# Last layer of a decoder: expert outputs scattered to their token's row, read back by plain reads, and the last unit finished tile by tile

## Chip, core and metric

One core of a Trainium2 chip runs the whole program. The metric is the device time of one execution in microseconds (us).

## The reference

A decoder of four layers, each of self-attention, cross-attention and an expert feed-forward, with a residual sum and a layer norm after each. There are 8 batches of 256 tokens, 2048 tokens of 256 float32 values. The change touches only the last part, the feed-forward of layer 3:

```python
x_flat = x.reshape(T, D)                                   # 2048 x 256
shared = jnp.einsum('th,hd->td', silu(x_flat @ shared_w1.T), shared_w2.T)   # hidden size 1024
gate_logits = x_flat @ gate_w.T                            # 8 experts
top_k_gates, top_k_idx = jax.lax.top_k(gate_logits, 2)
top_k_gates = jax.nn.softmax(top_k_gates, axis=1)
...
selected = jnp.einsum('ted,te->td', expert_out, gates)     # two chosen experts per token
x = _layernorm(x + shared + selected)
```

## The kernel before

`experts_sparse` computes the shared expert for all tokens and each of the 8 experts only for the tokens that chose it. The work is a list of 31 units q. A unit multiplies 256 rows with the up weights (four PSUM banks, 48 matmuls on line 3308, each float32 product made of three products of a high and a low part), applies silu (ScalarE), splits the result into high and low parts hH and hL (VectorE; in the last units ScalarE makes hH), and multiplies with the down weights (48 matmuls, line 3334) into a bank named y.

- Units 0 to 3 are the shared expert on batches 0 to 3. While they run, VectorE works out the routing: `choose`, `place`, `mark_tiles`, `mark_slots`, `find_tokens`. Each of a token's two choices gets a slot in one of 23 blocks of 256 slots; 32 small products on TensorE (`sources`, line 3269) turn that around into a list of the token of each slot.
- Units 4 to 26 are the 23 blocks, each with the weights of one expert. POOL gathers the rows of a block with two indirect DMAs (`fetch`, line 3453). VectorE copies the finished y to SBUF (`take_y`, line 3629) and SP stores it as a whole in DRAM in the order of the slots (`store_block`, line 3216).
- Units 27 to 30 are the shared expert on batches 4 to 7 ("late" units).

The weights of a unit (two loads of 1 MB by SP, up and down) are also split: ScalarE writes the high parts upH and downH (lines 3352, 3358), POOL the low parts upL and downL (`low`, lines 3441, 3444). SP starts the load of the weights after next when the low part has been made.

At the end each token needs its two block rows back. POOL waits until all blocks are stored, then issues 32 indirect gathers by slot (line 3483), one per tile of 128 tokens and choice, four to a batch. On VectorE `complete(b)` waits for a batch's four gathers, adds the rows with their gate weights (lines 3606, 3607) and makes the layer norm's statistics; POOL makes the power for the deviation (`power`, line 3473), ScalarE applies both in `finish(b)` (lines 3374, 3379), and SP stores the batch (line 3230). The batches are completed in pairs after the splits of units 28, 29 and 30 (`completed`), and batches 6 and 7 after unit 30's y has been taken:

```python
take_y(NQ - 1)
freed(dve, ("y", NQ - 1))
for b in range(2 * (B - FRONT - 1), B):
    complete(b)
```

All engines run their own program in order; the order is written out by hand, with semaphores between the engines. A wait holds all that stands behind it on that engine.

Of the kernel before, what the change touches and what calls it, by code (L numbers as in the profile page):

```python
# [3085 lines left out]
class Sparse:  # L3086


    def __init__(self, nc, g, scope, other, raw):
# [12 lines left out]
        self.yg = [raw[i // 16][:, D * (i % 16):D * (i % 16 + 1)] for i in range(2 * NT)]  # L3102
# [22 lines left out]
        self.source = sb("slot_tokens", TILES, U32)  # L3125
        self.chosen = sb("chosen", 136, BF16)
# [5 lines left out]
def experts_sparse(nc, g, name, n, scope):  # L3132
# [10 lines left out]
    rows_x, slots_y = g.dram["rows_x"], g.dram["slots_y"]  # L3143
# [15 lines left out]
    def completed(l):  # L3159

        return range(2 * (l - 1), 2 * l) if 1 <= l < B - FRONT else range(0)
# [11 lines left out]
    for q in range(NQ):  # L3173
        for f in range(4):
            u.add(("u", q, f), f)
        if q == 0:
            u.add("tokens", 6), u.add("rank", 7), u.add("count", 6)
        if q == FRONT - 1:
            u.add("source", 7)
        if q + 1 < NQ and block_of(q + 1) is not None:  # L3180
            u.add(("xT", q + 1), 6 + q % 2)
        u.add(("y", q), 4 + q % 2)

# [12 lines left out]
    with nc.Block() as block:  # L3196
        @block.sync
        def _(sp):
# [15 lines left out]
            def store_block(j):  # L3214
                freed(sp, ("y", FRONT + j))
                sp.dma_start(slots_y[j * S:(j + 1) * S, :].rearrange("(t p) d -> p t d", p=P), m_.yb[j % 2].rearrange("p (t d) -> p t d", d=D))\
                    .then_inc(g.block_stored[j % 2].sem, 16)
# [10 lines left out]
            for b in range(B):  # L3228
# [3 lines left out]
            sp.wait_ge(g.out_stored.sem, 16 * B)  # L3232

        @block.tensor
        def _(pe):
# [56 lines left out]
            for q in range(NQ):  # L3292
# [32 lines left out]
                split(pe, g.down_low, w)  # L3325
                to = claim(("y", q))
# [12 lines left out]
        def _(act):  # L3339
# [56 lines left out]
            for q in range(NQ):  # L3396

                after = weights_of(q) + 1 if last_unit(weights_of(q)) == q and weights_of(q) + 1 < SETS else None
                hidden(q, 0)
                hidden(q, 1)  # L3400
                if q == 2:
                    act.wait_ge(g.places_ready.sem, g.places_ready.base + 1)
                    nc.scalar.activation(m_.tile_row.rearrange("p (i c) -> p i c", c=2 * TILES)[:, :, 0:TILES],
                                         m_.at_tile.rearrange("p (i c) -> p i c", c=TILES), ACT.Copy, scale=m_.row).then_inc(g.places_ready.sem, 1)
# [19 lines left out]
            for b in range(2 * (B - FRONT - 2), B):  # L3424
                finish(b)

        @block.gpsimd
        def _(pool):
# [42 lines left out]
            def power(b):  # L3471
                pool.wait_ge(g.var_ready.sem, g.var_ready.base + b + 1)
                nc.gpsimd.tensor_tensor(g.rstd[:, 2 * b:2 * b + 2], g.vare[:, 2 * b:2 * b + 2], g.mhalf[:, 0:2], ALU.pow).then_inc(g.rstd_ready.sem, 1)


            split(pool, g.up_low, SETS - 1)
            split(pool, g.down_low, SETS - 1)
            for parity in range(2):
                sig = g.block_stored[parity]
                pool.wait_ge(sig.sem, sig.base + 16 * ((SLOTS + 1 - parity) // 2))  # L3480
# [7 lines left out]
            for b in range(2, B):  # L3488
                power(b)

        @block.vector
        def _(dve):
# [65 lines left out]
            def mark_tiles():  # L3558
# [18 lines left out]
            def find_tokens():  # L3577
# [4 lines left out]
                                                    in1=m_.found[:, 0:TILES], op1=ALU.add))  # L3582
                nc.vector.tensor_copy(m_.source[:, :], m_.token).then_inc(g.slots_ready.sem, 1)
# [19 lines left out]
            def add_choices(t):  # L3603

                r = rows(t)
                step(nc.vector.scalar_tensor_tensor(out=r, in0=m_.yg[2 * t], scalar=w1[:, t:t + 1], op0=ALU.mult, in1=r, op1=ALU.add))  # L3606
                nc.vector.scalar_tensor_tensor(out=r, in0=m_.yg[2 * t + 1], scalar=w2[:, t:t + 1], op0=ALU.mult, in1=r, op1=ALU.add)\  # L3607
                    .then_inc(g.added.sem, 1)

            def complete(b):  # L3610
                dve.wait_ge(g.gathered[b].sem, g.gathered[b].base + 64)
                add_choices(2 * b)
                add_choices(2 * b + 1)
                dve.wait_ge(g.added.sem, g.added.base + 2 * b + 2)
                normalize_part1(nc, g, dve, lambda t: rows(2 * b + t), 2, 2 * b, step, None)
                nc.vector.tensor_scalar(g.negmax[:, 2 * b:2 * b + 2], g.meanvar[:, 4 * b:4 * b + 4].rearrange("p (t two) -> p t two", two=2)[:, :, 0],
                                        -1.0, None, ALU.mult).then_inc(g.centered.sem, 1)

            def take_y(q):
# [5 lines left out]
                else:  # L3625
                    if j >= 2:
                        sig = g.block_stored[j % 2]
                        dve.wait_ge(sig.sem, sig.base + 16 * (j // 2))
# [3 lines left out]
            for q in range(NQ):  # L3632
# [19 lines left out]
                if q + 1 < NQ and block_of(q + 1) is not None:  # L3652
# [3 lines left out]
                        .then_inc(g.freed[u.bank(key)].sem, 1)  # L3656
                for b in completed(late(q)):
# [323 lines left out]
def decoder(nc, dram, out, order):  # L3981
# [3 lines left out]
    dram["slots_y"] = nc.dram_tensor("slots_y", (SLOTS * S, D), F32, kind="Internal").ap()  # L3985
# [213 lines left out]
```

## Time and profile before

| | us |
|---|---|
| median of three runs | 3414.25 |
| lowest, highest | 3413.76, 3416.06 |
| profiled execution, first to last instruction (span) | 3419.0 |
| TensorE busy in the span | 3115.7 (91%) |
| VectorE, ScalarE, POOL busy | 1875.7, 1705.1, 1520.5 |

Of the profiled execution only the span is known; it is 4.75 us longer than the median of the runs without a profile. Times in the rows count from the span's start. The feed-forward of the last layer takes from about 2980 to the end. PE is TensorE, PEld its weight loads, DVE VectorE, ACT ScalarE, POOL GpSimd, SPq the queue of SyncE.

### The profile page before, as it was taken

How to read it: one execution, taken by the hardware profiler on the slowest of the kernel's cores; microseconds unless marked ns; L12 is line 12 of the kernel's file. 1: busy time of each engine (PE TensorE's matmuls, PEld its weight loads, DVE VectorE, ACT ScalarE, POOL GpSimd, SP SyncE). 2: the span in 40 equal slices, each digit the busy share in tenths (PEclk: the TensorE clock that was granted, in tenths of full speed). 3: DMA queues.
4: the chain of work that ended last, by engine and by line, in shares of the span. 5: the costliest groups of instructions: out<-in, count | busy, mean ns of one | idle time of the engine just before them, and what ended most of it. 6: DMA issues, size and time to landing. Idle time of an engine off the chain costs nothing. (4 is left out here: it accounts for less than half of the span.)

```text
span 3419.0 us, 59989 instructions
## 1 busy us (share of the span) xinstructions
PE 3115.7 (91%) x23982; PEld 2628.8 (77%) x23993; DVE 1875.7 (55%) x3913; ACT 1705.1 (50%) x3695; POOL 1520.5 (44%) x1146
## 2 busy tenths in 40 slices
PE   6997999999698898998997989799997999889995
PEld 5776888888575565897665868678886888789995
DVE  4764222223566465776554754467775666565554
ACT  4763332332276554554654653356665666535553
POOL 0222344434212675674234651233334454539984
PEclk9998999999799999999998999899999999999998
DMA  1002000100000010442001010110001000036652
GB/s 65 3 11 79 19 19 19 38 1 1 23 3 23 1 50 1 149 168 75 3 3 43 8 50 1 39 50 1 1 1 38 6 6 1 26 115 217 223 181 74
DMA packets 49794, 156.96 MB, mean 46 GB/s; under 512 B 9322, under 2 KB 29438, under 8 KB 37104
## 3 DMA queue, kind: packets, MB, share of 16 engines
q1 hardware_dynamic: 45776, 142.90, 12.2%
q0 software_dynamic: 3744, 10.23, 1.0%
q8 instruction: 194, 3.18, 0.4%
q14 instruction: 80, 0.66, 0.1%
HBM read 142.06 MB, written 10.26 MB: 45 GB/s over the span
## 5 line engine op out<-in xcount | busy, mean ns | idle before, releaser
L1303 POOL TENSOR_TENSOR prob<-prob,inv 128x512 f32<-128x512 f32 x320 | 331.6, 1042 | 401.3 <-DVE inv L1355 391.8
L1193 ACT ACTIVATE prob<-banks,nmax 128x256 f32<-128x256 f32 x640 | 297.3, 474 | 155.1 <-DVE nmax L1349 155.0
L2682 POOL TENSOR_TENSOR hL<-product,hH 128x512 fp32r<-128x512 f32 x128 | 165.9, 1296 | 321.5 <-ACT hH L2629 321.5
L2288 DVE TENSOR_REDUCE nmax<-banks 128x4 f32<-128x1024 f32 (+1 forms) x192 | 217.5, 1133 | 153.7 <-PE banks L1870 85.9
L2727 DVE TENSOR_TENSOR product<-banks,silu 128x512 f32<-128x512 f32 x128 | 88.6, 692 | 388.6 <-PE banks L2553 333.4
L2621 ACT ACTIVATE silu<-banks 128x512 f32<-128x512 f32 x128 | 76.5, 598 | 367.6 <-PE banks L2553 367.6
L1349 DVE TENSOR_REDUCE nmax<-banks 128x2 f32<-128x512 f32 x320 | 215.4, 685 | 20.6 <-PE banks L1172 16.2
L2553 PE MATMUL banks<-xH,upH 128*128 128x512 f32 x512 | 202.1, 395 | 5.8 <-POOL upL L2669 5.8
L2553 PE MATMUL banks<-xL,upH 128*128 128x512 f32 x512 | 201.5, 394 | 0.0
L2553 PE MATMUL banks<-xH,upL 128*128 128x512 f32 x512 | 199.9, 390 | 0.0
L3364 ACT ACTIVATE banks<-banks 128x512 f32<-128x512 f32 x124 | 71.9, 584 | 213.9 <-PE banks L3308 186.8
L1093 PE MATMUL bank<-ident,prob 128*128 128x128 f32 x1280 | 167.8, 274 | 6.6 <-POOL prob L1303 6.6
L1093 PEld LDWEIGHTS bank<-ident,prob 128*128 128x128 f32 x1280 | 148.9, 141 | 21.8 <-issue 4.9
L2158 POOL TENSOR_TENSOR res<-res,bcast 128x512 f32<-128x512 f32 x16 | 21.4, 1337 | 313.7 <-DVE res L2356 313.7
L2105 ACT ACTIVATE probT<-banks 128x1024 f32<-128x1024 f32 (+1 forms) x129 | 123.2, 955 | 71.0 <-PE banks L1988 39.8
L3308 PE MATMUL banks<-xH,upH 128*128 128x256 f32 x496 | 142.7, 288 | 7.7 <-issue 7.7
L3308 PE MATMUL banks<-xH,upL 128*128 128x256 f32 x496 | 142.4, 287 | 6.7 <-issue 6.5
L3334 PE MATMUL bank<-downH,hH 128*128 128x256 f32 x496 | 143.7, 290 | 4.4 <-DVE hL L3648 4.3
L3308 PE MATMUL banks<-xL,upH 128*128 128x256 f32 x496 | 142.8, 288 | 3.2 <-issue 3.2
L2571 PE MATMUL bank<-downH,hL 128*128 128x256 f32 x512 | 144.9, 283 | 0.0
L2571 PE MATMUL bank<-downL,hH 128*128 128x256 f32 x512 | 144.8, 283 | 0.0
L2571 PE MATMUL bank<-downH,hH 128*128 128x256 f32 x512 | 144.4, 282 | 0.0
(617 smaller groups left out, 11026.6 us busy)
## 6 DMA issues: line engine op xcount, KB each, us to landing
W<-in_L_ffn_experts SPq DMA_DIRECT2D x80, 1024.0 KB, 5.4
W<-in_L_ffn_experts SPq DMA_DIRECT2D x8, 1536.0 KB, 7.9
slots_y<-W SPq DMA_DIRECT2D x23, 256.0 KB, 6.1
W<-strips SPq DMA_DIRECT2D x4, 768.0 KB, 7.5
W<-in_L_ffn_experts SPq DMA_DIRECT2D x9, 256.0 KB, 4.9
X<-in_x SPq DMA_DIRECT2D x1, 2048.0 KB, 8.3
cs<-in_ctxT SPq DMA_DIRECT2D x16, 128.0 KB, 2.3
W<-in_L_ffn_experts SPq DMA_DIRECT2D x1, 2048.0 KB, 7.6
```

Source lines behind the costliest of these rows:

```text
L1093: mm = nc.tensor.transpose(to[:, kt * S + qt * P:kt * S + (qt + 1) * P], m_.prob[p % 2][:, c0:c0 + P], ident[:, :])
L1193: ins = nc.scalar.activation(m_.prob[p % 2][:, e * 512 + j * S:e * 512 + (j + 1) * S], bank(key)[:, j * S:(j + 1) * S], ACT.Exp, bias=m_.n ...
L1303: nc.gpsimd.tensor_tensor(pr, pr, m_.inv[:, slot(p, e):slot(p, e) + 2].unsqueeze(2).to_broadcast([P, 2, S]), ALU.mult)\
L1349: nc.vector.tensor_reduce(m_.nmax[:, slot(p, e):slot(p, e) + 2], sc, AX.X, ALU.max, negate=True).then_inc(g.max_ready.sem, 1)
L2105: nc.scalar.activation(heads(m_.probT[(8 * b + i) % 3]), heads(g.pairs[1]), ACT.Exp)\
L2288: nc.vector.tensor_reduce(m_.nmax[b % 2][:, 2 * parts * i_:2 * parts * (i_ + 1)].rearrange("p (e q) -> p e q", e=2), scores.rearrange("p e ...
L2553: mm = nc.tensor.matmul(to[:, :], w_[e % 2][:, c0:c0 + P], x_[:, x0:x0 + 512], start=(at == 0), stop=(at == 5))
L2571: mm = nc.tensor.matmul(to, h_[:, c0:c0 + P], w_[e % 2][:, f * D:(f + 1) * D], start=(f == 0 and t % 2 == 0 and at == 0), stop=(f == 3 and ...
L2682: nc.gpsimd.tensor_tensor(m_.hL[:, at], m_.product[s % 2][:, :], m_.hH[:, at].bitcast(F32), ALU.subtract).then_inc(g.h_low.sem, 1)
L2727: nc.vector.tensor_tensor(m_.product[s % 2][:, :], bank(("u", s))[:, :], m_.silu[s % 2][:, :], ALU.mult)\
L3308: mm = nc.tensor.matmul(to[:, (f % 2) * S:(f % 2 + 1) * S], w_[w % 2][:, kk * 1024 + f * P:kk * 1024 + (f + 1) * P], x_[:, x0:x0 + S], sta ...
L3334: mm = nc.tensor.matmul(to[:, t * D:(t + 1) * D], h_[:, c0:c0 + P], w_[w % 2][:, f * D:(f + 1) * D], start=(f == 0 and t == 0 and at == 0) ...
```

## The change

1. **Scatter instead of store.** The list of slots gives for each slot its place as well, token + 2048 x choice (empty slots go to 128 spare rows). `mark_tiles` and `find_tokens` work this out. SP's store of a block and POOL's 32 gathers go. For each block POOL issues two indirect scatters, `scatter(j, 0)` and `scatter(j, 1)`, from SBUF to `rows_y` in DRAM. Each waits until the one before has landed.
2. **Plain reads.** When the last scatter has landed, SP issues sixteen reads of 256 KB, two for a batch, into the space of the weights.
3. **downL to VectorE.** The low part of the down weights is made by VectorE after its splits of a unit, no longer by POOL.
4. **Order of the end.** Batch 0 is completed in unit 27, 1 and 2 in unit 28, 3 and 4 in 29, 5 and 6 in 30. In unit 30 TensorE makes the down products one tile of 128 tokens after the other, in two banks. VectorE has the choices of the last two tiles added beforehand and finishes each tile with `end_tile`; SP stores the two tiles apart.
5. **ScalarE** no longer makes a factor of the routing product in unit 2; VectorE makes it.

The diff, cut to its core:

```diff
-        return range(2 * (l - 1), 2 * l) if 1 <= l < B - FRONT else range(0)
+        return range(max(2 * l - 1, 0), 2 * l + 1) if 0 <= l < B - FRONT else range(0)
...
+            def load_choices(b):
+                for k in range(2):
+                    sp.dma_start(m_.yg[b][:, 2 * k * D:2 * (k + 1) * D].rearrange("p (t d) -> p t d", d=D),
+                                 rows_y[k * T + b * S:k * T + (b + 1) * S, :].rearrange("(t p) d -> p t d", p=P)).then_inc(g.gathered[b].sem, 16)
             for w in range(1, SETS):
                 load_weights(w)
-                if w >= 4:
-                    store_block(w - 4)
-            for j in range(SETS - 4, SLOTS):
-                store_block(j)
+            split(sp, g.up_low, SETS - 1)
+            split(sp, g.down_low, SETS - 1)
+            for parity in range(2):
+                sig = g.block_stored[parity]
+                sp.wait_ge(sig.sem, sig.base + 32 * ((SLOTS + 1 - parity) // 2))
+            for b in range(B):
+                load_choices(b)
...
+                if q == NQ - 1:
+                    for t, key in enumerate((("y", q), "last")):
+                        to = claim(key)
+                        for f in range(8):
...
+                        done(key, mm)
+                    continue
...
-                split(pool, g.down_high, w)
-                nc.gpsimd.tensor_tensor(m_.downL[w % 2][:, :], raw[w % 2][:, 2048:4096], m_.downH[w % 2][:, :].bitcast(F32), ALU.subtract)\
-                    .then_inc(g.down_low.sem, 1)
+            def scatter(j, t):
+                if t == 0:
+                    freed(pool, ("y", FRONT + j))
+                    if j:
+                        sig = g.block_stored[(j - 1) % 2]
+                        pool.wait_ge(sig.sem, sig.base + 32 * ((j + 1) // 2))
+                else:
+                    sig = g.block_stored[j % 2]
+                    pool.wait_ge(sig.sem, sig.base + 32 * (j // 2) + 16)
+                i = 2 * j + t
+                nc.gpsimd.indirect_dma_start(rows_y, bass.IndirectOffsetOnAxis(ap=m_.place[:, i:i + 1], axis=0),
+                                             m_.yb[j % 2][:, t * D:(t + 1) * D], None).then_inc(g.block_stored[j % 2].sem, 16)
...
             for w in range(1, SETS):
                 low(w)
+                if w >= 3:
+                    scatter(w - 3, 1)
                 if w + 1 < SLOTS:
                     fetch(w + 1)
+                if w >= 2:
+                    scatter(w - 2, 0)
+            scatter(SLOTS - 1, 1)
...
-            for t in range(NT):
-                for k in range(2):
-                    nc.gpsimd.indirect_dma_start(m_.yg[2 * t + k], None, slots_y,
-                                                 bass.IndirectOffsetOnAxis(ap=m_.slots[:, k * NT + t:k * NT + t + 1], axis=0))\
-                        .then_inc(g.gathered[t // 2].sem, 16)
-                if t in (9, 11):
-                    power(t // 2 - 4)
...
-                for k in range(2):
-                    half = slice(k * NT, (k + 1) * NT)
-                    nc.vector.tensor_tensor(each(m_.tile_row, 2 * TILES)[:, half, TILES:2 * TILES], each(m_.at_tile, TILES)[:, half, :],
-                                            m_.count[:, 0:NT].unsqueeze(2).to_broadcast([P, NT, TILES]), ALU.mult)
+                nc.vector.tensor_scalar(m_.offset[:, :], m_.low, m_.row, None, ALU.subtract)
+                step(nc.vector.tensor_scalar(m_.choice[:, :], m_.count[:, 0:2 * NT], float(2 * NT), None, ALU.subtract))
+                for part, factor in enumerate((m_.offset, m_.choice)):
+                    ins = nc.vector.tensor_tensor(each(m_.tile_row, 2 * TILES)[:, :, part * TILES:(part + 1) * TILES], each(m_.at_tile, TILES),
+                                                  factor[:, :].unsqueeze(2).to_broadcast([P, 2 * NT, TILES]), ALU.mult)
+                ins.then_inc(g.places_ready.sem, 1)
...
-                nc.vector.tensor_copy(m_.source[:, :], m_.token).then_inc(g.slots_ready.sem, 1)
+                step(nc.vector.tensor_scalar(m_.token, m_.token, m_.row, float(2 * T), ALU.add, ALU.add))
+                step(nc.vector.tensor_copy(m_.place[:, :], m_.token))
+                nc.vector.tensor_scalar(m_.source[:, :], m_.place[:, :], T - 1, None, ALU.bitwise_and).then_inc(g.slots_ready.sem, 1)
...
+            def end_tile(t, key, n_):
+                filled(dve, key)
+                step(nc.vector.tensor_tensor(rows(t), bank(key)[:, 0:D], rows(t), ALU.add))
+                normalize_part1(nc, g, dve, lambda _: rows(t), 1, t, step, None)
+                dve.wait_ge(g.rstd_ready.sem, g.rstd_ready.base + n_ + 1)
+                normalize_part2(nc, g, lambda _: rows(t), 1, t, lambda _: g.X[:, t * D:(t + 1) * D]).then_inc(g.x_done.sem, 1)
...
+                after = next_weights(q)
+                if after is not None:
+                    split(dve, g.down_high, after)
+                    nc.vector.tensor_tensor(m_.downL[after % 2][:, :], raw[after % 2][:, 2048:4096], m_.downH[after % 2][:, :].bitcast(F32), ALU.subtract)\
+                        .then_inc(g.down_low.sem, 1)
                 for b in completed(late(q)):
                     complete(b)
-            take_y(NQ - 1)
-            freed(dve, ("y", NQ - 1))
-            for b in range(2 * (B - FRONT - 1), B):
-                complete(b)
+            dve.wait_ge(g.gathered[B - 1].sem, g.gathered[B - 1].base + 32)
+            for t in (NT - 2, NT - 1):
+                step(add_choices(t, g.X[:, t * D:(t + 1) * D]))
+            end_tile(NT - 2, ("y", NQ - 1), B - 1)
+            end_tile(NT - 1, "last", B)
```

## Rows read from the trace of the kernel before

**Rows 1.** The page's first line.

```profile
span 3419.0 us, 59989 instructions
```

**Rows 2.** Windows, units 27 to 30: busy us by engine, TensorE clock, DMA share, GB/s.

```profile
3329.86:3341.38 11.52, 11.52 (x99) 11.52 (x98) 3.37 (x5) 4.33 (x8) 8.95 (x8) 1.00 0.26 81
3341.38:3371.44 30.06, 16.50 (x99) 14.95 (x98) 6.49 (x17) 4.15 (x8) 13.21 (x15) 0.72 0.23 66
3371.44:3383.34 11.90, 11.78 (x98) 11.58 (x98) 8.74 (x22) 7.70 (x16) 9.67 (x10) 1.00 0.29 79
3383.34:3401.60 18.26, 13.85 (x96) 13.08 (x95) 10.55 (x34) 8.12 (x18) 5.81 (x8) 0.91 0.26 80
```

**Rows 3.** Chain that ended last, 3330 to the end: start us, us, what.

```profile
3335.62 5.76 PE bank L3334 x48
...
3356.23 2.43 issue
...
3390.00 5.58 PE banks L3308 x35
...
3413.12 0.40 ACTq L3196
```

**Rows 4.** POOL's timeline, first and last of the twenty and of the twelve gathers.

```profile
3333.75 0.96 POOL L3483 DMA_INDIRECT W<-slots_y,slots  x1 [0.74 <-POOL downL L3444]
...
3357.54 0.95 POOL L3483 DMA_INDIRECT W<-slots_y,slots  x1 [0.30 <-issue]
3371.38 0.97 POOL L3473 TENSOR_TENSOR rstd<-vare,mhalf 128x2 f32<-128x2 f32 x1 [12.89 <-DVE vare L307]
3372.53 1.03 POOL L3483 DMA_INDIRECT W<-slots_y,slots  x1 [0.19 <-issue]
...
3387.67 0.96 POOL L3483 DMA_INDIRECT W<-slots_y,slots  x1 [0.30 <-issue]
```

**Rows 5.** Timelines of VectorE and ScalarE: what ended their long waits.

```profile
3360.10 0.69 DVE L3624 TENSOR_TENSOR W<-bank,X 128x512 f32<-128x512 f32 x1 [22.03 <-remote]
...
3362.29 1.07 ACT L3364 ACTIVATE banks<-banks 128x512 f32<-128x512 f32 x2 [25.06 <-remote]
```

**Rows 6.** Windows: plain traffic at its thickest, and one block unit.

```profile
2183.00:2186.00 3.00, 3.00 (x19) 2.88 (x18) 0.69 (x1) 1.17 (x2) 0.14 (x1) 0.76 1.06 388
...
3246.40:3258.35 11.95, 11.95 (x103) 11.95 (x102) 6.72 (x10) 6.35 (x7) 11.15 (x5) 1.00 0.67 218
```

**Rows 7.** VectorE's timeline in mark_tiles.

```profile
3027.29 1.69 DVE L3565 TENSOR_TENSOR W<-W 128x1472 bf16<-128x1472 f32 x1
3029.01 1.76 DVE L3570 TENSOR_TENSOR W<-W 128x736 bf16<-128x736 bf16 x2
```

**Rows 8.** DMA issues, last number us to landing: whole program; 3330 to 3340.

```profile
slots_y<-W SPq DMA_DIRECT2D x23, 256.0 KB, 6.1
...
slots_y<-W SPq DMA_DIRECT2D x1, 256.0 KB, 2.1
```

**Rows 9.** Groups on POOL, 3060 to 3330.

```profile
L3441 POOL TENSOR_TENSOR upL<-W,upH 128x2048 fp32r<-128x2048 f32 x23 | 106.7, 4638 | 12.2 <-ACT upH L3352 12.1
```

**Rows 10.** Timelines: VectorE beside a POOL operation and without one; a later gather.

```profile
1834.61 2.76 DVE L1400 TENSOR_TENSOR woL<-W,woH 128x1024 fp32r<-128x1024 f32 x1 [4.47 <-ACT woH L1243]
...
1833.91 2.36 POOL L1280 TENSOR_TENSOR wvL<-W,wvH 128x1024 fp32r<-128x1024 f32 x1
...
2610.18 1.23 DVE L1400 TENSOR_TENSOR woL<-W,woH 128x1024 fp32r<-128x1024 f32 x1 [1.70 <-ACT woH L1243]
...
3382.26 1.13 POOL L3483 DMA_INDIRECT W<-slots_y,slots  x1 [0.30 <-issue]
```

**Rows 11.** VectorE's timeline: last splits of unit 27; complete(5), and what follows it.

```profile
3336.78 1.29 DVE L3648 TENSOR_TENSOR hL<-banks,hH 128x512 fp32r<-128x512 f32 x2 [0.75 <-ACT hH L3368]
...
3401.15 0.48 DVE L3606 SCALAR_TENSOR_TENSOR W<-W,small 128x256 f32<-128x256 f32 x1
...
3404.37 0.68 DVE L3624 TENSOR_TENSOR W<-bank,X 128x512 f32<-128x512 f32 x1
```

More of the change, by code:

```diff
@@ L3100, in __init__ @@
         self.yb = [other[:, 5120:5632], other[:, 5632:6144]]
-        self.yg = [raw[i // 16][:, D * (i % 16):D * (i % 16 + 1)] for i in range(2 * NT)]
+        self.yg = [raw[b // 4][:, 4 * D * (b % 4):4 * D * (b % 4 + 1)] for b in range(B)]
         self.xbH, self.xbL = ([a.rearrange("p (k t) -> p k t", k=2)[:, :, i * S:(i + 1) * S] for i in range(2)] for a in (g.xH, g.xL))
@@ L3125, in __init__ @@
         self.source = sb("slot_tokens", TILES, U32)
+        self.place = sb("slot_places", TILES, U32)
+        self.offset, self.choice = sb("row_offsets", 2 * NT, F32), sb("choice_tiles", 2 * NT, F32)
         self.chosen = sb("chosen", 136, BF16)
@@ L3182, in experts_sparse @@
         u.add(("y", q), 4 + q % 2)
+    u.add("last", 4 + NQ % 2)
     def bank(key):
@@ L3222, in _ @@
                 load_weights(w)
-                if w >= 4:
-                    store_block(w - 4)
-            for j in range(SETS - 4, SLOTS):
-                store_block(j)
+            split(sp, g.up_low, SETS - 1)
[5 more added lines that the diff above has]
+                load_choices(b)
             out = g.dram["out"]
-            for b in range(B):
+            for b in range(B - 1):
                 sp.wait_ge(g.finished.sem, g.finished.base + b + 1)
@@ L3325, in _ @@
                 split(pe, g.down_low, w)
+                if q == NQ - 1:
+                    for t, key in enumerate((("y", q), "last")):
+                        to = claim(key)
+                        for f in range(8):
+                            if t == 0 and f % 2 == 0:
+                                freed(pe, ("u", q, f // 2))
+                            c0 = f * S + t * P
+                            for at, (h_, w_) in enumerate(((m_.hH, m_.downH), (m_.hH, m_.downL), (m_.hL, m_.downH))):
+                                mm = nc.tensor.matmul(to[:, 0:D], h_[:, c0:c0 + P], w_[w % 2][:, f * D:(f + 1) * D],
+                                                      start=(f == 0 and at == 0), stop=(f == 7 and at == 2))
+                        done(key, mm)
+                    continue
                 to = claim(("y", q))
@@ L3423, in _ @@
                     down_high(after)
-            for b in range(2 * (B - FRONT - 2), B):
+            for b in completed(B - FRONT - 1):
                 finish(b)
@@ L3467, in _, with power @@
                 low(w)
+                if w >= 3:
+                    scatter(w - 3, 1)
                 if w + 1 < SLOTS:
                     fetch(w + 1)
[L3471 to L3480, printed above, removed]
-            for t in range(NT):
-                for k in range(2):
-                    nc.gpsimd.indirect_dma_start(m_.yg[2 * t + k], None, slots_y,
-                                                 bass.IndirectOffsetOnAxis(ap=m_.slots[:, k * NT + t:k * NT + t + 1], axis=0))\
-                        .then_inc(g.gathered[t // 2].sem, 16)
-                if t in (9, 11):
-                    power(t // 2 - 4)
-            for b in range(2, B):
-                power(b)
+                if w >= 2:
+                    scatter(w - 2, 0)
+            scatter(SLOTS - 1, 1)
+            def power(i, t0, tiles):
+                pool.wait_ge(g.var_ready.sem, g.var_ready.base + i + 1)
+                nc.gpsimd.tensor_tensor(g.rstd[:, t0:t0 + tiles], g.vare[:, t0:t0 + tiles], g.mhalf[:, 0:tiles], ALU.pow).then_inc(g.rstd_ready.sem, 1)
+            for b in range(B - 1):
+                power(b, 2 * b, 2)
+            power(B - 1, NT - 2, 1)
+            power(B, NT - 1, 1)
         @block.vector
@@ L3601, in rows, with add_choices @@
                 return m_.R[:, t * D:(t + 1) * D]
[L3603 to L3608, printed above, removed]
+            def add_choices(t, onto):
+                r, yg = rows(t), m_.yg[t // 2]
+                first, second = (yg[:, (2 * k + t % 2) * D:(2 * k + t % 2 + 1) * D] for k in range(2))
+                step(nc.vector.scalar_tensor_tensor(out=r, in0=first, scalar=w1[:, t:t + 1], op0=ALU.mult, in1=onto, op1=ALU.add))
+                return nc.vector.scalar_tensor_tensor(out=r, in0=second, scalar=w2[:, t:t + 1], op0=ALU.mult, in1=r, op1=ALU.add)
             def complete(b):
[L3611 to L3614, printed above, removed]
+                dve.wait_ge(g.gathered[b].sem, g.gathered[b].base + 32)
+                add_choices(2 * b, rows(2 * b))
+                step(add_choices(2 * b + 1, rows(2 * b + 1)))
                 normalize_part1(nc, g, dve, lambda t: rows(2 * b + t), 2, 2 * b, step, None)
```

26 lines of the change are left out of this document (12 added, 14 removed).

## Prediction

> **What bounds the kernel now.** I began with the page's span [rows 1] and cut the end of the last layer into its units with the windows view [rows 2]. In the twenty-three block units before it TensorE is busy all the time: 11.95 us of each 11.95 [rows 6]. The first of the four last units, 27, still takes 11.52 us. Then unit 28 takes 30.06, unit 29 11.90, and unit 30 with what follows it 18.26; busy time is only 16.50 of the 30.06, and the granted clock falls to 0.72. Against 11.52 for a unit, unit 28 loses 18.5 us.
>
> The chain of waits says how [rows 3]. TensorE leaves the down products of unit 27 on time, and then its matmuls come one by one with up to 2.43 us of "issue" between them: it waits for nothing that the profile shows. The timeline of POOL shows what runs beside it [rows 4]: twenty indirect gathers, one each 1.25 us from 3333.75 to 3358.5. TensorE flows again only when ScalarE wakes, at 3362.3 [rows 5]. A second run of twelve gathers, 3372.53 to 3388.6, has the same beside it: single matmuls until 3390.00, where the next full piece of the chain begins, which ends at 3395.6. VectorE and ScalarE are late by the same wait [rows 5]: they wait 22.03 and 25.06 us for signals of TensorE and wake at 3360.10 and 3362.29, though unit 27's products were over at 3341.4. So the stall is on TensorE's side, and it lasts as long as the gathers. TensorE loses time in two places: 18.5 us in unit 28, and 6.5 us in the up products of unit 30 (3383.34 to 3395.6, where 5.76 is usual); unit 29 loses 0.4. Together 25.4 us.
>
> **The change part by part.**
>
> *Gathers out, plain reads in.* The 32 gathers at the end (4.2 MB) go, and sixteen reads of 256 KB from SP take their place. What plain traffic does to TensorE is read where it is thickest while TensorE works: at 2183 to 2186 the DMA engines are full (share 1.06, 388 GB/s), and TensorE is busy 3.00 of 3.00 us while its clock is just rising (0.76 granted) [rows 6]. In a block unit 218 GB/s cost nothing. So I price the stall in the new kernel at 0; the other end is that the reads hold TensorE back while they run, 4.2 MB at 388 GB/s = 11 us. I take 0, since these rows are of the same queue and kind. That gives TensorE 25.4 us back; how much reaches the end is worked out below.
>
> *When the reads come.* Unit 26's products end at 3329.86 [rows 2] and are taken 0.7 us later, two scatters follow each other's landing (the store without other traffic lands in 2.1 us [rows 8]), so SP starts its reads near 3339, and the first batch's two land by 3341.9. VectorE is done with unit 27 at 3338.07 [rows 11] and waits in complete(0) some 4 us. Behind it stand take_y(27) and the splits of unit 28, which TensorE wants only from 3347; the delay is hidden, with nearly 1 us to spare. If the reads came 5 us later, TensorE would pay about 4.
>
> *Tiles of the routing.* mark_tiles has at_tile of 1472 elements at 1.69 us and two halves of 736 in 1.76 together, with the other factor done by ScalarE. Now VectorE makes two products of 1472: 3.4 us for 1.76, and two small steps of 0.17 [rows 7]. VectorE runs without a gap there up to the mark that the source products of TensorE wait for, so all of it is on the path: +2.0 us. Two more small steps in find_tokens, 0.4 us, delay the first fetches, which land before unit 3's up products end: 0 to 0.4.
>
> *downL to VectorE.* 23 subtractions leave POOL, each the size of the one that takes 4.64 us [rows 9]. On VectorE 1024 elements took 1.23 us with POOL idle [rows 10], so 2048 take 2.3. VectorE is busy 6.72 of 11.95 us in a block unit; 9.0 still fit, and the new work stands behind its splits and before take_y, whose bank is one of two. Nothing of it is on the path.
>
> *Scatters in a loop with POOL.* This is the term with two sides. Each unit POOL now has upL (4.64 us [rows 9]), scatter (j,1), two fetches, and scatter (j+1,0), which waits until scatter (j,1) has landed; the next upL stands behind it. The loop is landing + 0.96 of issue [rows 4] + 4.64 + 0.2 for two signals (an estimate) = landing + 5.8. It may take 11.95. A transfer queued beside a 1 MB weight load landed in 6.1 us (median of 23 stores), without one in 2.1 [rows 8]. SP issues the next weights right beside scatter (j,1), so 6.1 is the nearer row: the loop is 11.9, equal to the unit. I take 0 cost, and keep +0.5 us a unit above (a landing of 6.6; 22 units less the 1.9 us by which upL is early now, an estimate from the timeline of such a unit: it ends near 10.0 us of the unit, and the next up products start at 11.95: +9) and nothing below, as TensorE is full.
>
> The Trainium skill, page "DMA: Bandwidth & Descriptors", section "Anatomy of one DMA — SWDGE (gpsimd) path", fits a GpSimd DMA at about 2.0 us and bytes over 436 GB/s, 2.3 us for a scatter's 128 KB; by that the loop would be an estimated 8.1 us and this risk gone. The rows differ: 2.1 us holds only with no load in the queues.
>
> *The end.* With no stall TensorE ends up products of unit 30 at 3329.86 + 3 x 11.52 + 5.76 = 3370.2, plus 2.0 for the routing = 3372.2. VectorE's splits end 2.45 us after the up products (3338.07 against 3335.62 in unit 27 [rows 3, 11]): 3374.6. Then it does complete(5) and (6), 3.22 us each (3401.15 to 3404.37 [rows 11]): 3381.1; the choices of the last two tiles, four of 0.48 to 0.49: 3383.1. Unit 30's products by tile end near 3375.5 and 3378.4, so TensorE no longer sets the end: VectorE does. A last tile costs the addition 0.48, its share of the statistics 0.9 (3.22 less four additions leaves 1.27 for two tiles), POOL's power 0.97 [rows 4], the normalisation 0.48: 2.8, twice, in series: 3388.7. From the last X to the end of the span are 5.5 us (ScalarE's last signal at 3413.52 [rows 3], span 3419.0): 3394.2.
>
> The sum: 3419.0 to 3394.2, -24.8 us, of the profiled execution. It is nearly the stall: what the tiles gain behind TensorE's last product pays for the +2.0. The profiled execution's span is 4.75 us longer than the median of 3414.25. If nothing of the stall is the profiler's, the time is 3414.25 - 24.8 = 3389.5; if these 4.75 us lie in the stall, it is 3394.2. I take 3392.
>
> **The rivals.**
>
> *The stall belongs partly to the profiled execution.* For it: only TensorE is held, which fills more of the records than any other engine, and the span is above the median. Without the stall the old order ends so: VectorE has complete(4) and (5) from 3372.6, take_y, complete(6) and (7), until 3386.5, ScalarE 1.9, then 5.5: 3394, as the new one. So the change would be worth nothing: 3414. Against it: the median is only 4.75 us under the span. A half-real stall gives 3402.
>
> *The reads hold TensorE as the gathers did*, for their 11 us: 3403. Rows 6 speak against it.
>
> *POOL becomes the bound.* One mechanism, on the other side: scatter (j,1) lands later than 6.1 us, and every unit grows. Each microsecond costs 22. The gain of 22 is eaten when the unit grows by 1.1 us, from a landing near 7.2; at 8 us the loop is 13.8: 22 x 1.85 - 1.9 = +39, and with the gain of 22 the time is 3431. For it: the store's 6.1 is a median under one load. Against it: the scatter stands in a queue of its own, ahead of the fetches.
>
> *The lock between VectorE and POOL.* With two SBUF inputs, a VectorE subtraction that began 0.7 us into a POOL one took 2.76 us, ending 1.1 after it [rows 10]; a gather that began beside a VectorE addition took 1.13 us where 0.95 is usual [rows 10, 4]. So downL starts when upL ends, and scatter (j,1), due at that instant, may wait its 2.3 us. The weight load ahead of it hides this as far as I can see; if not, the loop is 14.2: 22 x 2.2 - 1.9 = +47, time 3439.
>
> The Trainium skill states such an exclusive lock in "SBUF — State Buffer", section "Who interferes with whom", for a VectorE instruction with two SBUF inputs against a GpSimd one that reads SBUF; by that rule the trace agrees for the subtraction.
>
> **How the numbers follow.** My forecast (gathers' stall gone, 3386 to 3398): 0.62. Stall partly or wholly the profiler's: 0.14, of which 0.10 without change. Reads hold TensorE: 0.06. POOL's loop costs under 15 us: 0.06, near the gain (no change) 0.03, more 0.05. The lock: 0.04. Faster by over 0.2% (6.8 us, about what a measurement of this kernel can tell): 0.62 + 0.04 + 0.06 + 0.05 = 0.77, lowered to 0.75 as these cases can add up; no change 0.14; slower 0.11. For 8 in 10 I leave out the slow loop and the lock above and little below: 3385 to 3414. The forecast's own range is 3386 to 3398.
>
> **What would show it.** Right: no "issue" waits of TensorE above 1 us after 3340; units 27 to 30 at 11.5 us each; sixteen reads from SP near 3341 that land by 3360; mark_tiles 2.0 us longer; VectorE as the last link, two single tiles in series at the end. POOL's upL begins as soon as upH is there (its wait names ScalarE): if its wait names a DMA, the loop has closed, and the block units show more than 11.95 us. VectorE's downL should last 2.3 to 3.2 us, the scatters 0.96 or, with the lock, up to 3.2. The prediction is wrong if plain reads stall TensorE, if the block units grow, or if the old stall was cheaper without the profiler.

## The result, and the profile after

| | before | after |
|---|---|---|
| median | 3415.15 (4 runs, 3413.76 to 3419.5) | 3450.5 (4 runs, 3443.09 to 3460.82) |
| profiled execution, span | 3419.0 | 3459.0 |
| last layer: SP's store of rows_x to the end of the span | 3419.0 - 2979.45 = 439.6 | 3459.0 - 2982.16 = 476.8 |

After over before is 1.0108, interval [1.0087, 1.0129]: the change made the kernel slower by 1.1%. In the profiled executions the last layer grew by 37.2 us. I forecast 24.8 less.

The first thing to see is where TensorE is busy. Windows of the kernel after: 240 us of block units, then most of the down products of unit 27 with the up products of unit 28, the next two such pairs, and the end (columns as in [rows 2]):

```profile
3060.00:3300.00 240.00, 212.76 (x1695) 210.18 (x1694) 201.99 (x188) 107.97 (x119) 168.52 (x81) 0.96 0.51 184
...
3401.18:3412.70 11.52, 10.20 (x87) 10.03 (x85) 5.62 (x16) 4.34 (x9) 1.04 (x2) 1.00 0.66 210
3412.70:3424.45 11.75, 11.75 (x98) 11.75 (x99) 9.33 (x28) 4.74 (x10) 1.63 (x2) 1.00 0.57 188
3424.45:3435.98 11.53, 11.53 (x98) 11.53 (x98) 9.39 (x28) 7.74 (x16) 1.62 (x2) 1.00 0.13 45
3435.98:3459.00 23.02, 6.02 (x48) 5.61 (x47) 12.86 (x41) 8.61 (x19) 2.95 (x4) 0.73 0.17 58
```

Behind the block units TensorE runs nearly as forecast. SP issues the sixteen reads from 3403.38 on, and beside them (210 and 188 GB/s in the window) TensorE is busy but for one wait of 1.3 us, which is for VectorE; before had 16.50 of 30.06 [rows 2]. But in the block units it is busy 212.76 of 240, where it was always busy [rows 6]. From one upL to the next, a **round** of POOL, are 14.82 us on average, not 11.95. Groups of the block units, 3060 to 3390, POOL and then VectorE (to be held against [rows 9]):

```profile
L3464 POOL TENSOR_TENSOR upL<-W,upH 128x2048 fp32r<-128x2048 f32 x23 | 109.8, 4772 | 8.0 <-ACT upH L3379 7.4
L3478 POOL DMA_INDIRECT rows_y<-W,slot_places x43 | 76.9, 1789 | 82.7 <-DMA rows_y<-W,slot_places 78.9 <-issue 3.8
```

```profile
L3699 DVE TENSOR_TENSOR downL<-W,downH 128x2048 fp32r<-128x2048 f32 x23 | 114.6, 4983 | 0.4 <-ACT downH L3385 0.4
```

POOL stands 78.9 us ahead of its scatters and the releaser is the landing of a scatter. Only 3 of the 23 upL still wait for upH (7.4 us together); in [rows 9] nearly all of POOL's wait ahead of them was for upH. A scatter takes 1.79 us on the mean, downL 4.98, where 0.96 and 2.3 were put in. The timelines show why. POOL:

```profile
3194.22 4.58 POOL L3464 TENSOR_TENSOR upL<-W,upH 128x2048 fp32r<-128x2048 f32 x1
3198.96 2.87 POOL L3478 DMA_INDIRECT rows_y<-W,slot_places  x1 [0.17 <-issue]
3202.14 0.98 POOL L3487 DMA_INDIRECT W<-rows_x,slot_tokens  x1 [0.30 <-issue]
3203.42 0.96 POOL L3487 DMA_INDIRECT W<-rows_x,slot_tokens  x1 [0.30 <-issue]
3207.96 1.01 POOL L3478 DMA_INDIRECT rows_y<-W,slot_places  x1 [3.58 <-DMA rows_y<-W,slot_places]
3209.00 5.87 POOL L3464 TENSOR_TENSOR upL<-W,upH 128x2048 fp32r<-128x2048 f32 x1
```

VectorE, and SP's weight loads, at the same time:

```profile
3193.70 7.25 DVE L3699 TENSOR_TENSOR downL<-W,downH 128x2048 fp32r<-128x2048 f32 x1
3208.22 2.28 DVE L3699 TENSOR_TENSOR downL<-W,downH 128x2048 fp32r<-128x2048 f32 x1
```

```profile
3198.96 0.33 SPq L3217 DMA_DIRECT2D W<-in_L_ffn_experts  x1
3201.12 0.33 SPq L3220 DMA_DIRECT2D W<-in_L_ffn_experts  x1
```

Read them side by side. downL starts while the scatter ahead of upL is still being issued, 0.5 us before upL, and ends only at 3200.95, 2.15 us after upL: nearly the whole of its 2.28 us was done when upL was over. So while upL ran, downL did not. Scatter (j,1), due at 3198.96, is in turn held until 3201.83. The end of downL also frees SP's down load, issued at 3201.12. So the scatter, whose issue is over at 3201.83, stands behind two loads of 1 MB; before, these were issued 4.6 us apart (SP at 3197.13 and 3201.74). The next scatter starts at 3207.96, 9.0 us after scatter (j,1) was due and 6.1 after its issue was over. Then 1.0 and upL, and the round has 14.8 us. In a few other rounds, as that of 3209, downL gets through first, upL takes 5.87, the scatter 1.0, and both loads are issued within 0.5 us; from this scatter to the next are 7.4 to 8.8 us. Over all rounds the median is 8.8. TensorE is late behind upL: the view of waits for 3060 to 3390 puts 42.4 us of "issue" ahead of its up products.

The end, VectorE's last tile and SP's last lines:

```profile
3449.19 0.42 DVE L3653 TENSOR_TENSOR W<-bank,W 128x256 f32<-128x256 f32 x1
...
3451.20 0.41 DVE L313 TENSOR_SCALAR X<-W,meanvar,rstd 128x256 f32<-128x256 f32 x1 [0.67 <-POOL rstd L3512]
```

```profile
3403.38 10.31 SPq L3225 DMA_DIRECT2D W<-rows_y  x16
3414.75 32.45 SPq L3242 DMA_DIRECT2D out<-X  x7
3449.31 2.69 SPq L3246 DMA_DIRECT2D out<-X  x2
```

From one last tile's X to the next are 2.33 us (3448.87 to 3451.20), where I put 2.8. But from the last X (3451.61) to the end are 7.4 us, not 5.5; the experiments show why.

### The profile page after: what moved, and what is told of

Same layout as the page of the kernel before. It is cut to its first block and busy times, and to the rows that moved or that the text cites. A ratio compares the mean times of both kernels' runs of the same rounds, so it can differ in the third digit from the quotient of the medians.

```text
span 3459.0 us, 60033 instructions
## 1 busy us (share of the span) xinstructions
PE 3127.8 (90%) x23993; PEld 2641.1 (76%) x23993; DVE 1995.3 (58%) x3945; ACT 1701.0 (49%) x3690; POOL 1467.1 (42%) x1137
## 5 line engine op out<-in xcount | busy, mean ns | idle before, releaser
L3323 PE MATMUL banks<-xH,upH 128*128 128x256 f32 x496 | 148.8, 300 | 42.4 <-issue 42.4
```

The lines of the kernel that those rows point to most:

```text
L3323: mm = nc.tensor.matmul(to[:, (f % 2) * S:(f % 2 + 1) * S], w_[w % 2][:, kk * 1024 + f * P:kk * 1024 + (f + 1) * P], x_[:, x0:x0 + S], sta ...
```

## The experiments

They ran in three groups on two chips. On these, 73 runs of before lie between 3378.5 and 3400.4, where the runs of the prediction and the result gave 3413.8 to 3419.5. Which chip those first runs used is not on record; below they are "the first chip", though it is not shown that the chip itself makes the difference. Ratios are each against before in the same group. The store of rows_x in the last layer comes at 2968.5 to 2982.2 us in the profiles, a spread of some 14 us that comes from the layers that are the same in all kernels. So beside the time stands the **stretch** of the profiled execution, from that store to the end of the span. Before has 414.2 and 414.2 on the two chips and the kernel after 476.8 and 473.7, so I take differences of 2 to 3 us between two stretches with care.

**e1_quarters: the lock split.** downL as four subtractions of 512 columns, so that POOL gets in between.

```diff
-                    nc.vector.tensor_tensor(m_.downL[after % 2][:, :], ...)
+                    for c in range(0, 2048, 512):
+                        ins = nc.vector.tensor_tensor(m_.downL[after % 2][:, c:c + 512], ...)
```

> Edit: VectorE makes downL in four pieces of 512 columns instead of one operation of 2048; all else as in the changed kernel. Lock theory (VectorE's downL keeps POOL's scatter (j,1) from starting, 2.87 us instead of 0.97 in most units, and this delay is what makes the loop longer than 11.95 us): a piece holds POOL back only about 0.6 us, the scatter takes at most 1.6 us, a block unit shrinks by 1.3 us or more, from 14.7 to 13.4 or less, and the time falls by 25 us or more, to 3425 or less. Queue theory (scatter (j,1) lands late because both weight loads of 1 MB, which SP now issues 2.2 us apart, are served before it): the scatter starts earlier but lands no earlier, units stay at 14.2 to 14.7, the time stays within 10 us of 3450.

Measured 3402.13 us, ratio 1.0043 [1.0026, 1.006]; stretch 423.8, round 12.39 us. Scatter (j,1) takes 1.3 us, and from its issue to the next scatter the median is 6.3 us, not 8.8. The lock theory had the direction, but this edit does not separate the two: the scatter's issue is now over before SP starts the down load (3166.79 against 3167.89 in one round), so one load less stands ahead of it as well.

**e2_down_late and e3_loads_late: the loads moved.** SP starts the down load (e2), or both (e3), only when scatter (j,1) has landed. downL is whole. The edit of e3; e2 has the same wait ahead of the down load instead:

```diff
+                if w >= 5:
+                    sp.wait_ge(g.block_stored[(w - 5) % 2].sem, g.block_stored[(w - 5) % 2].base + 32 * ((w - 5) // 2 + 1))
                 sp.dma_start(raw[w % 2][:, 0:2048], src[:, 0:2048])...
```

> Edit: SP issues the down load only when scatter (j,1) has landed; the up load as in the changed kernel. Queue theory: one load of 1 MB stands before the scatter instead of two, it lands 1.5 to 2.5 us earlier counted from its issue (now 9.0), a block unit takes 12.2 to 13, the time is 3400 to 3415. Lock theory: the scatter still takes 2.87 us and the units stay above 14, time about 3445.

> Edit: SP issues both weight loads only when scatter (j,1) has landed. Queue theory: nothing stands before the scatter; with the lock's 1.9 us it lands some 4.5 to 5.5 us after its issue, POOL's loop is 10.3 to 11.2 us, less than TensorE's 11.95, so the block units go back to 11.95 to 12.1 us and the time is 3385 to 3400, faster than the kernel before. Lock theory: the lock alone keeps the units above 14 us, time about 3445. The loads then stand 5 us later in the unit; if they come too late for ScalarE's upH, POOL's upL waits for ScalarE and the units lie between, 12.2 to 13.

e2: 3396.93, ratio 1.0035 [1.0025, 1.0044], stretch 424.0, round 12.31; a scatter still takes 2.9 us (median) but the next one starts 6.0 after it. The lock theory had units above 14 here and is refuted in that form. e3: 3388.45, ratio 1.001 [0.9999, 1.0021], stretch 416.4, round 11.95; 3.3 us (median) to the next scatter. With both loads out of the way TensorE is full, though VectorE and POOL still hold each other up. Windows of e3:

```profile
3060.00:3300.00 240.00, 240.00 (x2011) 240.00 (x2010) 198.09 (x221) 127.32 (x141) 180.97 (x100) 1.00 0.60 218
```

**e8_two_tables: the loop opened.** Scatters (j,0) and (j,1) write two tables, so each waits for the landing of one a whole unit before. The order on every engine and the places of the scatters and loads stay; VectorE's take_y waits for both tables' scatters. The kernel leaves out the joining of the two tables: the reads at the end fetch rows of x.

```diff
-                    if j:
-                        sig = g.block_stored[(j - 1) % 2]
-                        pool.wait_ge(sig.sem, sig.base + 32 * ((j + 1) // 2))
+                sig = g.block_stored[t]
+                if j:
+                    pool.wait_ge(sig.sem, sig.base + 16 * j)
...
+                nc.gpsimd.indirect_dma_start((rows_y, rows_z)[t], ...)
```

> The changed kernel, but scatter (j,0) writes one table and scatter (j,1) another, so that each waits only for the landing of the one a whole unit before; the lock, the place of the scatters in the queues and the loads' times are as in the changed kernel. Left out: the reads at the end fetch rows of x in place of the experts' rows. Theory 'closed loop' (what costs is the wait for scatter (j,1)'s landing ahead of upL): POOL's round is 4.6 + 2.9 + 1.9 + 1.0 = 10.4 us and some waits, the block units are 11.95 us again, though scatter (j,1) still lands 8 to 9 us after its issue; some 55 to 63 us less than the changed kernel, ratio near 1.000. Rival 'lock' (POOL and VectorE, each blocked by the other, are full by themselves): the units stay above 12.5 us. Rival 'traffic': TensorE waits for weights whose loads are slowed by the scatters, units above 12.5 us with waits that name the loads.

Measured 3388.55, ratio 1.0003 [0.999, 1.0015]; stretch 415.0, round 11.95. One round of POOL in e8, and the transfers of 3060 to 3300 (last number: us from issue to landing):

```profile
3190.23 4.63 POOL L3464 TENSOR_TENSOR upL<-W,upH 128x2048 fp32r<-128x2048 f32 x1 [0.43 <-ACT upH L3379]
3195.03 2.87 POOL L3475 DMA_INDIRECT rows_z<-W,slot_places  x1 [0.17 <-issue]
3198.20 0.98 POOL L3484 DMA_INDIRECT W<-rows_x,slot_tokens  x1 [0.30 <-issue]
3199.48 0.96 POOL L3484 DMA_INDIRECT W<-rows_x,slot_tokens  x1 [0.30 <-issue]
3200.75 1.01 POOL L3475 DMA_INDIRECT rows_y<-W,slot_places  x1 [0.30 <-issue]
```

```profile
rows_y<-W,slot_places POOLq DMA_INDIRECT x20, 4.3
rows_z<-W,slot_places POOLq DMA_INDIRECT x19, 8.1
```

The scatter is still held to 2.87 us and still lands 8.1 us after it was due; the unit costs nothing. So neither the lock nor the traffic is a bound by itself. They cost because upL stands behind a wait for the landing they delay. In e8 the loads are still issued 2.1 us apart, but from 3060 to 3300 what ends POOL's idle time ahead of upL is upH again (21 times, 0.43 us in the round shown). The wait went, and 58.7 us of stretch with it (473.7 in r_after, 415.0 here). This settles the cause.

**r_before, r_before2, e5_before_plain: the stall at the gathers.** The kernel before on both chips, and before with sixteen plain reads from SP in place of POOL's 32 gathers (each token gets other tokens' rows: the permutation is left out).

> The kernel before itself, looked at on the chip that runs the others, since the last chip's runs of it had a median 27 us below the first chip's. Theory 1 (the 32 gathers hold TensorE back in every execution): unit 28 takes about 30 us and TensorE waits with 'issue' between single matmuls beside the twenty gathers; the stretch from SP's store of rows_x in the last layer to the end is near 440 us. Theory 2 (the stall is not there on every chip; the run with plain reads in place of the gathers was no faster than before because there was no stall to remove): units 27 to 30 take 11.5 to 12 us each with the gathers running beside them, and the stretch is 410 to 414 us.

> The kernel before once more, to see on what the stall of TensorE beside the gathers hangs. On two chips after the first (medians 3387.4 and 3390.4; the second of them also profiled) it was absent; the first chip's four runs of before lie at 3413.8 to 3419.5. If the stall belongs to the first chip, a run elsewhere has units 27 to 30 at 11.5 us and a span near 3390; if it comes and goes, this one may have unit 28 at 30 us and a span near 3415.

> The kernel before with one edit: the 32 indirect gathers at the end are replaced by sixteen plain reads of 256 KB from SP, which read the block rows as they lie, so each token gets rows of other tokens (this part of the computation is left out); POOL has only the powers left. It prices the gathers' stall of TensorE without the profiler and without scatters. If the stall is real: TensorE runs through units 27 to 30 at 11.5 us each, and the time is 3386 to 3396 (20 to 28 us less). If the stall belonged to the profiled execution, or plain reads stall TensorE too: within 7 us of 3414, and in the second case single matmuls with issue waits appear beside the reads.

Windows of r_before, units 27 to 29 (where [rows 2] have 11.52, 30.06 and 11.90), and its first gathers:

```profile
3327.86:3339.38 11.52, 11.52 (x99) 11.52 (x98) 3.36 (x5) 4.33 (x8) 8.95 (x8) 1.00 0.25 80
3339.38:3350.90 11.52, 11.52 (x99) 11.52 (x98) 6.50 (x17) 4.33 (x8) 8.78 (x10) 1.00 0.36 103
3350.90:3362.42 11.52, 11.52 (x99) 11.52 (x98) 9.37 (x28) 6.83 (x14) 9.18 (x10) 1.00 0.39 121
```

```profile
3331.75 0.96 POOL L3483 DMA_INDIRECT W<-slots_y,slots  x1 [0.74 <-POOL downL L3444]
3333.02 0.95 POOL L3483 DMA_INDIRECT W<-slots_y,slots  x1 [0.30 <-issue]
```

The same gathers at the same pace, and TensorE loses nothing. r_before2 shows the same on the other chip. The stretch is 25.4 us shorter than on the first chip, which is what I had read as the stall's size. With no stall to remove, e5 measured 3384.52, ratio 0.9994 [0.9982, 1.0006]. That is close to the 3386 to 3396 that I had expected for a real stall, but only because before itself is at 3387.41 here. The stretch of e5 is 409.2, 5.0 under before: 2.6 of them are POOL's shorter last drain (see e6 below), and 2.4 were already there when TensorE ended its last product.

**r_after.**

> The changed kernel itself on the same chip as the others. If the loop over POOL, the scatter's landing and the weight loads is its whole loss, the block units are again near 14.8 us instead of 11.95 (22 x 2.85 = 63 us), and it stands 63 us above the version whose loads wait (which measured 3388): some 3450 us, ratio 1.018 to 1.019, where before has no stall to give back; ratio 1.010 again, if before has the stall of 25 us on this chip. A rival, that the first chip's runs of after were slow for a reason of their own, expects the ratio between 1.00 and 1.008.

3447.6 us (4 runs), ratio 1.017 [1.0149, 1.0191], stretch 473.7, round 14.66. The changed kernel is as slow here as on the first chip (3450.5); only before differs.

**e6_root, e7_root_order, e7_again, e9_before_root: the end of the span.** Every profile so far ended with a last instruction on POOL, a drain, that starts with its last power (TENSOR_TENSOR below). Records of SP and POOL in the kernel after (start us, us, engine, instruction):

```
3450.58 8.188 GpSimd DRAIN
3450.62 0.553 GpSimd TENSOR_TENSOR
3453.53 0.013 Sync DRAIN
```

SP woke from the last output at 3453.53 and POOL's drain ends at 3458.77, 0.2 us before the span does; these 5.2 us are POOL's alone. Behind its last power the drain took 3.88 us in e5 (46 indirect transfers of this layer), 6.49 in before (78), 7.64 in after (92): (7.64 - 3.88) / 46 = 0.082 us for each transfer. In e6 to e9 a square root on ScalarE and a reciprocal on VectorE replace the last powers, so POOL ends with the power of batch 5.

```diff
-            power(B - 1, NT - 2, 1)
-            power(B, NT - 1, 1)
...
+                nc.scalar.activation(g.rstd[:, t0:t0 + tiles], g.vare[:, t0:t0 + tiles], ACT.Sqrt).then_inc(g.sort_step.sem, 1)
...
+                nc.vector.reciprocal(g.rstd[:, t0:t0 + tiles], g.rstd[:, t0:t0 + tiles]).then_inc(g.rstd_ready.sem, 1)
```

> The version with both loads late; and POOL's last three powers (batch 6 and the last two tiles) are replaced by a square root on ScalarE and a reciprocal on VectorE, so that POOL's last work is the power of batch 5. In every profile so far the span ends when a last drain of POOL ends, which starts with its last power and took 4.57 us (46 indirect transfers issued by POOL in the program's last layer), 7.19 (78) and 8.19 (92): 0.08 us for each transfer and 0.9 more; SP was done 0.4, 3.0 and 5.3 us before the end. Theory 'drain': it now starts about 6.5 us earlier relative to the last X, still takes 8.2, and the span ends within 1 us of SP's last wake: 3.5 to 5 us less than with the loads late alone (ratio 0.9995 to 1.000 where that had 1.001). Rival 'the end waits for SP or for the outputs' landing': the drain ends 5.3 us after SP again and the time stays.

> As the one before, with downL in four pieces of 512 and, in the last round of POOL's loop, scatter(21,1) ahead of upL of the shared weights. The last three scatters end some 2.5 us earlier, so complete(0) waits 2 us less and no longer delays the hL of unit 28, which held TensorE 1.3 us: 1 to 2 us less than the one before. If the scatter ahead of upL delays the up products of unit 27 by more than that (its wait for the landing of scatter(21,0) was 2.2 us), it is the same or 1 us more.

> The best version so far once more on another chip or day: both loads late, pieces, square root on ScalarE, last scatter ahead of upL. It measured 0.998 [0.9968, 0.9991] against before; here 0.997 to 0.999 where before has no stall beside its gathers, 0.990 to 0.992 where it has.

> The kernel before, changed only at its last two normalisations: the powers of batches 6 and 7 are a square root on ScalarE and a reciprocal on VectorE, so that POOL's last work is the power of batch 5. Theory 'drain': POOL's last drain still takes 6.5 us after its last power (78 transfers), but it is over before SP's last output has landed, and the span ends within 0.5 us of SP's last wake instead of 3.0: 2 to 3 us less, ratio 0.999 to 0.9995. Rival: the drain waits for the outputs, no change.

| | median, ratio | stretch |
|---|---|---|
| e6: e3 and the root | 3386.56, 0.9993 [0.9981, 1.0006] | 411.0 |
| e7: e6, downL in pieces, scatter(21,1) ahead of upL | 3383.34, 0.998 [0.9968, 0.9991] | 409.4 |
| e7 again, other chip | 3384.17, 0.9983 [0.9972, 0.9995] | 409.5 |
| e9: before and the root | 3386.82, 0.9994 [0.9983, 1.0004] | 410.3 |

In all four the drain keeps its length behind the power (7.63 or 6.49 us) but is over before SP wakes, and the span ends 0.2 us behind SP. e6's stretch is 5.4 us under e3's, of which 5.2 are the drain.

e9's stretch is 4.0 under before's. The span now ends 0.2 us behind SP's wake and not 3.2, which is 3.0 us for the drain. The other 1.0 is not the root's. Counted from the store, TensorE ended its last product 2.1 us earlier than in r_before, and 1.6 of that was there at the first fetch, up to which the two programs do the same work. What differed was the granted clock in the routing, here 28 to 36 us after the store (r_before, then e9):

```profile
3005.49:3013.49 8.00, 8.00 (x57) 8.00 (x57) 3.10 (x10) 0.58 (x1) 0.00 (x0) 0.81 0.00 0
2998.95:3006.95 8.00, 8.00 (x67) 8.00 (x66) 4.08 (x15) 0.91 (x2) 0.00 (x0) 0.96 0.00 0
```

e5's profile has the same lead (0.99 in these 8 us); the three of before have not, and whether that is chance is open. From TensorE's last product to the last X are 13.4 us in e9 and 12.3 in before, so its root chain is 1.1 us longer than POOL's powers, not shorter.

e7 is the best version: about 0.2% faster than before in both runs, and 4.8 us in the stretch. What the scatters and the new end are worth by themselves where the gathers do not stall is small and not well known. Against e9 as it was profiled it is 0.8 us; if e9's lead of 2.1 us is chance, it is about 3 (an estimate). The medians of e7 and e9 in the same group are 2.7 us apart, where single runs of either spread over 8 to 11. e7 was not run on the first chip.

## Why the prediction was wrong

**The step that failed is POOL's loop.** I wrote "the loop is 11.9, equal to the unit. I take 0 cost". The formula, landing + 5.8, was right: 9.0 + 5.8 = 14.8 is the round shown above. The landing was mis-sized: 6.1 taken, 8.8 (median) measured from the time the scatter was due. 6.1 was the store's median under one load. That 6.1 is also about the time behind the end of the issue, under two loads, is chance; the lock's 1.9 us came on top; where the scatter was not held, it stood behind two loads issued together. Two things were in reach. First, I moved downL to VectorE in one part and let SP's loads stay 4.6 us apart in the other, though the down load waits for downL: the move itself put the two loads side by side. Second, I had named the lock at 14.2 us a unit and dismissed it with "the weight load ahead of it hides this"; the load does not hide it, as SP issues the other load the moment downL lets go. The rival "POOL becomes the bound" had the mechanism (8 us: 3431), the lock rival nearly the size (3439); but the slow cases of the first got 0.05 of chance, and the lock 0.04. They were not two rivals but one chain: e2 takes one load from ahead of the scatter and leaves 12.31, e1 takes one load and most of the hold out and leaves 12.39, and e8 with all links but the wait in place costs nothing. A loop that closes at 11.9 of 11.95 should have got most of the chance.

The size, in the two profiled executions on the first chip: from the first upL of the blocks to the last the kernel after takes 334.3 us and before 274.5, +59.8. From the store to that first upL it is +1.8, and from the last upL to the end of the span 71.0 against 95.3, -24.3. Together 37.3, the measured growth but for rounding. In r_after the blocks take 331.0, so some 3 us of the loop's cost vary. The part behind the blocks gave about the 24.8 that I had forecast; the loop, which I had put at 0, took more than twice that.

**The stall** is absent from the kernel after, and plain reads cost TensorE nothing: right in size on the first chip. That the gathers were its cause is argued, not shown: no run there took out the gathers alone. What was not seen is that it is no property of the kernel. The rival "the stall belongs partly to the profiled execution" looked in the wrong place: the first chip's times of before (median 3415.15) are 25 to 28 us above the medians elsewhere (3387.4 to 3390.4), not only its profiled execution, and elsewhere the stall is absent with and without the gathers.

**Reads and complete(0).** SP's reads started 2.9 us after the last scatter's start, and VectorE waited 5.7 us in complete(0), not 4. "Nearly 1 us to spare" was short: TensorE waited 1.3 us for hL at 3412.70. The last scatters had themselves been late, since scatter (21,1) was held 2.86 us by downL.

**Routing.** mark_tiles made two products of 1.69 us; from the store of rows_x to the first fetch are 66.5 us, 64.8 before: +1.8, forecast 2.0 to 2.4.

**The end.** Up products of unit 30 over to the span's end: 23.0 us in after, 22.0 forecast. A tile was 0.5 us cheaper than put; the 5.5 us "from the last X to the end" were no constant. They are POOL's drain, which grew with 14 more indirect transfers and now starts 1.0 us before the last X (3450.58, 3451.61) where it started 1.9 before it (3411.62, 3413.52).

**The chances.** In the sum for "faster", 0.05 stands where the loop's 0.06 belongs (0.78 for 0.77); nothing hangs on it. What counts is that slower had 0.11.

**Landing and lock beside the pages.** The last scatter of the kernel after, with no load in the queues, landed in 2.4 us; with two loads ahead it took 8.1 (e8). The fit of the Trainium skill, page "DMA: Bandwidth & Descriptors", section "Anatomy of one DMA — SWDGE (gpsimd) path", gives an estimated 2.3 us for 128 KB; the trace agrees for the empty queue alone, and for the loop it was farther off than my 6.1. The exclusive lock that the Trainium skill states in "SBUF — State Buffer", section "Who interferes with whom", agrees with the 7.25 us of downL. The trace goes further: an indirect DMA's issue on POOL is held as well, 2.87 us for 1.0.

## What to carry to other kernels

Before a wait for a DMA's landing is put into a loop of an engine, write down what is issued in the microseconds ahead of that DMA, by every queue, in the new order and not the old; a landing read from the old trace belongs to the old order. If the loop comes out equal to the period, count it as closed, and break it (another table, an older landing to wait for, the loads behind it) before pricing the rest. Of a stall that has no releaser in the profile, ask for the same kernel on another chip before building a change on it. And before a part of a microsecond or two is given to an edit, compare the stages that the edit did not touch: in e9 they were 1.6 us ahead, at a higher granted clock.

## What was unexpected of the hardware

- The stall beside the gathers is in the one trace from the first chip, and the times of all four runs of before there fit it; two traces and 73 times from the other two chips are without it. Within it TensorE's records (weight loads and matmuls) stand on a grid of 0.70 us (3357.26, 3358.66, 3359.38, 3360.08, 3360.78, 3361.48), as if single instructions came to it at that pace. Its cause stays open: no run here met it again. The one 16 KB packet of the instruction queue at that time (3340.31) took 0.96 us, as such packets do in r_before (0.98 to 1.13), so the trace shows no slow fetch of instructions.
- An engine's last drain can end the span: on POOL 3.88, 6.49 and 7.64 us behind its last work with 46, 78 and 92 indirect transfers in the layer, which is 0.082 us for each. It was hidden where POOL's last work came early (e6, e7, e9).
- A VectorE subtraction of two SBUF tiles and one of POOL don't run side by side: one of the two gets through and the other is longer by its wait (downL 7.25 us for 2.28, or upL 5.87 for 4.6). Which of them differs from round to round, and even the issue of an indirect DMA waits (2.87 us for 1.0).
